# Cross-attention key loop: full-height matmuls on a block-diagonal query matrix, or 64-row tiles in pairs

## Chip, cores and metric

The kernel runs on one core of a Trainium2 chip. The metric is the device time of one execution in microseconds.

## The reference

One Perceiver-like layer on `x` [1, 128, 256], with a context of 12544 rows of 256. It has four parts. The first is nearly all of the time.

```python
q = LN(x) @ Wq.T + bq; k = ctx @ Wk.T + bk; v = ctx @ Wv.T + bv      # 128 queries, 12544 keys
scores = einsum('bhqd,bhkd->bhqk', q * 0.25, k)                      # 16 heads of 16
x += softmax(scores) @ v @ Wo.T + bo
x += linear attention of LN(x) (feature map exp / x + 1, gate)       # 128 x 256
x += causal attention with RMS norm and rope, then its MoE (8 experts, top 2, silu gate)
```

All in fp32.

## The kernel before

The context comes transposed, in 49 steps of 256 keys (`SK`). Matrices are split into a high and a low part in fp32r, and each projection is the sum of three products (high x high, low weight x high, high x low context).

For a step n the order of work is:

- `context_high(n)` (ScalarE, line 363) rounds the context to fp32r, `context_low(n)` (GpSimd, line 316) takes the rest.
- `keys(n, ...)` (TensorE, line 556) gives the keys in `k_bank`: 12 matmuls of 128x128 weights and 256 columns. `values(n, ...)` (line 567) gives the values in `v_bank`, 12 too.
- `keys_high(n)` (ScalarE, line 373) and `keys_low(n)` (VectorE, line 930) split the keys into `kst`. Six DMAs of SP (`keys_place`, line 244) lay them into a ring `kT`, so that each pair of heads takes 128 rows: 64 rows a head, of which 16 hold the high part, 16 the low part, 16 the high part again and the rest ones.
- `values_out(n)` copies the values into a ring `val`. This is ScalarE's in the first steps (line 383), VectorE's from then on (line 940).
- `max_scores(n, p)` (TensorE, line 584), for each of 8 pairs of heads: two matmuls with `qM`, one for each head. `qM` holds a head's 64 rows and zeros in the other 64. VectorE reduces the 512 results of a pair to two maxima per query (`step_max`, line 946). The two maxima banks are used in turn.
- A block is 4 steps. After its last step `block_max(b)` reduces the steps' maxima, `turn_max(b)` transposes them on TensorE into `k_bank`, VectorE's `max_turned(b)` copies them into `maxT`, and two small DMAs of SP (`max_rows`, line 257) put them, negated and in two parts, into rows of the query matrix `qmat[b % 2]`. So the scores come with the block's maximum subtracted.
- `scores(n, q)` (TensorE, line 608) runs `LAG` = 5 steps behind the maxima: 8 units of two matmuls of 256 columns, each with keys as weights and two heads of `qmat` (half zeros) as moving data. Three score banks are used in turn. ScalarE takes the exponential of a unit (`exponential`, line 403).
- `weighted_values(n, j)` (TensorE, line 624) adds the weighted values: 64 matmuls a step with 17 columns of weights (16 values and a one), four of them beside each other in columns of the array.

The order on TensorE is written out in the loop over t (lines 690 to 719): eight turns q, each with one scores unit, one maxima unit and half a projection; after the second turn stand the weighted values of the step before. In steps 49 to 53 only scores, weighted values and the turning of the blocks' parts (`turn_part`, line 647) are left. SP's order is that of lines 274 to 286: a context load, the rows of a finished block (`max_rows`), then `keys_place(t + 2)`, which waits for the slot of the ring to be free. Each engine and each queue works strictly in order.

After the loop come the merge of the 12 blocks' parts, and the small layers (lines 720 on), which the change does not touch.

Of the kernel before, what the change touches and what calls it, by code (L numbers as in the profile page):

```python
# [27 lines left out]
RING = 7  # L28
VRING = 8
CRING = 4  # L30
GROUPS = 4
# [25 lines left out]
def last_step(b):  # L57
# [11 lines left out]
    "v_done",  # L69
    "val_ready",  # L70
# [34 lines left out]
def perceiver_layer(nc, dr, out):  # L105
    ctx = ExitStack()
    with ctx:
# [43 lines left out]
        qmat = [place(f"qmat{i}", [P, PAIRS, 2, P], F32R) for i in range(2)]  # L151
        qM = place("qM", [P, PAIRS, 2, P], F32R)
# [49 lines left out]
        B = [ctx.enter_context(nc.psum_tensor(f"bank{i}", [P, 512], F32)) for i in range(8)]  # L202
        k_bank, v_bank, mx_bank, sc_bank, pv_bank = B[0], B[1], B[2:4], B[4:7], B[7]

# [19 lines left out]
        def _(sp):  # L224
# [23 lines left out]
            def max_rows(b):  # L248
# [6 lines left out]
                for a in range(2):  # L255
                    row = 64 * a + 3 * HD
                    sp.dma_start(qmat[b % 2][row:row + 2, :, a, :].bitcast(F32),
                                 maxT[2 * PAIRS * a:2 * PAIRS * (a + 1), :].bitcast(F32)
                                 ).then_inc(S["max_rows"], 16)
# [14 lines left out]
            for t in range(-2, NS + 1):  # L274
                if CRING <= t + 6 < NS:
                    ctx_load(t + 6)
                for b in range(NB):
                    if t == last_step(b) + 1:
                        max_rows(b)
                if t + 2 < NS:  # L280
                    keys_place(t + 2)
# [5 lines left out]
                if t == NS - 2:  # L287

                    sp.wait_ge(S["v_done"], 2 * NS)
# [22 lines left out]
        def _(pool):  # L312
# [6 lines left out]

            def key_ones(r):  # L320
# [3 lines left out]
            def queries(b):  # L324
# [4 lines left out]
                pool.tensor_copy(qmat[b][:, :, :, :], qM[:, :, :, :]).then_inc(S["pool_qmat"], 1)  # L329
# [4 lines left out]
            pool.memset(qM[:, :, :, :].bitcast(F32), 0.0)  # L334
# [4 lines left out]
            for t in range(-2, NS):  # L339
                if t + 3 < NS:  # L340
                    context_low(t + 3)
# [15 lines left out]
        def _(act):  # L357
            def context_high(n):

                act.wait_ge(S[f"ld_ctx{n % CRING}"], 16 * (n // CRING) + 16)  # L360
                if n >= 2:
                    act.wait_ge(S["v_done"], 2 * (n - 2) + 2)
# [14 lines left out]
            def values_out(n):  # L377


                act.wait_ge(S["v_done"], 2 * n + 2)  # L380
# [24 lines left out]

            def part_out(b):
# [17 lines left out]
            for a in range(2):  # L424
                rows = slice(64 * a, 64 * a + 64)
                last = act.activation(qM[rows, PAIRS // 2:PAIRS, a, :],
                                      mx_bank[1][rows, :].rearrange("p (h q) -> p h q", q=P), ACT.Copy)
            last.then_inc(S["act_q0"], 1)
# [4 lines left out]
            for t in range(LAST + 2):  # L433
                if t == NS:
# [4 lines left out]
                for q in range(8):  # L439
                    n = t - LAG  # L440
                    if 0 <= n < NS:
                        exponential(n, q)
                    if q == 0 and t + 2 < NS:
                        keys_high(t + 2)
                    if q == 5 and t + 2 <= LAG:
                        values_out(t + 2)
                    if q == 5 and t + 4 < NS:
                        context_high(t + 4)
                    if q == 2:
                        for b in range(NB):  # L450
                            if n - 1 == last_step(b) and t != NS:
                                part_out(b)
# [69 lines left out]
        def _(pe):  # L522
# [16 lines left out]
            def keys(n, t, half):  # L539

                if (t, half) == (0, 0):
# [4 lines left out]
                    if n >= 1:  # L546
                        turned = [b for b in range(NB) if last_step(b) == n - 4]
                        if turned:
                            pe.wait_ge(S["mt_read"], turned[0] + 1)
                        else:  # L550
                            pe.wait_ge(S["kl_ready"], n)
# [9 lines left out]
            def values(n, j, half):  # L561
# [7 lines left out]
                if half == 1:  # L569
# [6 lines left out]
            def max_scores(n, p):  # L576

                m = 8 * n + p
                if m >= 2:
                    pe.wait_ge(S["mx_read"], m - 1)  # L580
                for a in range(2):
                    if p == 2 and a == 1 and n + 3 < NS:
                        pe.wait_ge(S["cl_ready"], n + 4)
                    last = pe.matmul(mx_bank[p % 2][:, a * SK:(a + 1) * SK], qM[:, p, a, :], kT[:, n % RING, p, :],  # L584
                                     start=True, stop=True)
                last.then_inc(S["mx_done"], 1)

            def turn_max(b):
# [3 lines left out]
                pe.wait_ge(S["kl_ready"], min(last_step(b) + 4, NS))  # L592
                pe.transpose(k_bank[:, 0:P].bitcast(F32R), maxparts[:, :, :, :].rearrange("q a s p -> q (a s p)"),
                             ident_r[:, :]).then_inc(S["mt_done"], 1)

            def scores(n, q):

                k, b, j, g = 8 * n + q, block_of(n), q // GROUPS, q % GROUPS
                if n == first_step(b) and q == 0:
                    pe.wait_ge(S["max_rows"], 32 * (b + 1))  # L600
                if k >= 3:
                    pe.wait_ge(S["exp_ready"], k - 2)
                for i in range(2):
                    p = 2 * g + i
                    if q == 0 and i == 1 and n + LAG < NS:

                        keys_placed(n + LAG)
                    last = pe.matmul(sc_bank[k % 3][:, i * 2 * P:(i + 1) * 2 * P], kT[:, n % RING, p, j * P:(j + 1) * P],  # L608
                                     qmat[b % 2][:, p, :, :], start=True, stop=True)
                last.then_inc(S["sc_done"], 1)  # L610
# [690 lines left out]
```

## Time and profile before

| | |
|---|---|
| runs | 575.61 us median of 3 (575.16 to 578.5) |
| profiled execution | span 577.4 us |
| TensorE matmuls busy | 544.8 us (94%) |
| VectorE / ScalarE / GpSimd busy | 421.6 / 330.7 / 92.1 us |
| granted TensorE clock | 0.985 of full on average |
| DMA | 70.41 MB, mean 122 GB/s |

Matmuls are pipelined: a matmul's shown duration (284 ns for 256 columns) holds its way through the array, and the distance between the starts of two tells what one costs the stream. TensorE's weight loads have rows of their own (PEld) and run beside the matmuls.

### The profile page before, as it was taken

The numbers are of one execution on the slowest core, as the hardware profiler recorded it, in microseconds if no ns is written. First come the engines' busy times: TensorE is split into PE (matmuls) and PEld (weight loads), VectorE is DVE, ScalarE is ACT, GpSimd is POOL, SyncE is SP. The second block draws the span as 40 slices with busy tenths as digits, with TensorE's granted clock in tenths as the row PEclk, the third lists the DMA queues.
The fourth block names the chain that finished last, engine by engine and source line by source line (L and its number), as shares of the span: only waits on it lengthen the run. The fifth ranks groups of instructions, "written<-read, shape, count | busy, mean of one in ns | idle before, by whom it ended". The sixth has DMA issues, their size and how long they took to land.

```text
span 577.4 us, 15741 instructions
## 1 busy us (share of the span) xinstructions
PE 544.8 (94%) x6460; PEld 502.4 (87%) x6460; DVE 421.6 (73%) x797; ACT 330.7 (57%) x635; POOL 92.1 (16%) x75
## 2 busy tenths in 40 slices
PE   7888989999999999999999999999998998778897
PEld 7777989999999999999999999999987877736686
DVE  5689868778777787787787877877877317866674
ACT  3423747667676676675666766766764850062463
POOL 7641101011011011110110111101000000015000
PEclk9999999999999999999999999999999999978899
DMA  6999995856977878777678787796575019920000
GB/s 196 152 158 152 182 154 97 120 119 120 129 120 115 128 121 124 118 113 129 119 114 128 121 122 118 120 125 101 78 118 175 3 38 377 375 87 1 1 1 9
DMA packets 44615, 70.41 MB, mean 122 GB/s; under 512 B 6784, under 2 KB 15104, under 8 KB 44416
## 3 DMA queue, kind: packets, MB, share of 16 engines
q1 hardware_dynamic: 44304, 69.02, 65.8%
q8 instruction: 50, 0.82, 0.8%
q10 hardware_dynamic: 240, 0.39, 0.5%
q14 instruction: 21, 0.17, 0.1%
HBM read 30.53 MB, written 0.13 MB: 53 GB/s over the span
## 4 chain that ended last, share of the span: by engine, by line
PE 80%; DVE 8%; DMA 6%; SPq 2%; ACT 1%; issue 1%; POOL 0%; DVEq 0%
PE bank L608 17%; PE bank L624 15%; PE bank L584 14%; PE bank L567 10%; PE bank L556 10%; DMA kT<-kst 5%; PE bank L834 3%; PE bank L850 3%; SPq L244 2%; PE bank L632 2%; DVE stepmax L946 1%; DMA qmat<-maxT 1%; PE bank L654 1%; PE bank L532 1%; PE bank L647 1%
## 5 line engine op out<-in xcount | busy, mean ns | idle before, releaser
L946 DVE TENSOR_REDUCE stepmax<-bank 128x2 f32<-128x512 f32 x392 | 262.9, 688 | 92.2 <-PE bank L584 68.7
L403 ACT ACTIVATE probs<-bank 128x512 f32<-128x512 f32 x392 | 229.8, 601 | 139.8 <-PE bank L608 135.6
L608 PE MATMUL bank<-qmat,kT 128*128 128x256 f32 x784 | 164.5, 294 | 4.2 <-DMA kT<-kst 3.4
L584 PE MATMUL bank<-kT,qM 128*128 128x256 f32 x784 | 161.2, 287 | 4.1 <-DVE stepmax L946 1.9
L608 PEld LDWEIGHTS bank<-qmat,kT 128*128 128x128 f32 x784 | 120.8, 191 | 18.9 <-issue 9.9
L584 PEld LDWEIGHTS bank<-kT,qM 128*128 128x128 f32 x784 | 121.5, 191 | 7.7 <-DVE stepmax L946 4.0
L316 POOL TENSOR_TENSOR cparts<-ctxT,cparts 128x512 fp32r<-128x512 f32 x49 | 63.4, 1294 | 326.7 <-ACT cparts L363 326.6
L556 PE MATMUL bank<-cparts,wk 128*128 128x256 f32 x588 | 101.3, 283 | 2.1 <-POOL cparts L316 2.1
L567 PE MATMUL bank<-wv,cparts 128*128 128x256 f32 x588 | 101.9, 284 | 0.7 <-ACT val L383 0.7
L624 PE MATMUL bank<-probs,val 128*17 128x128 f32 x3136 | 95.1, 273 | 0.0
L624 PEld LDWEIGHTS bank<-probs,val 128*17 128x17 f32 x3136 | 81.4, 97 | 6.5
L556 PEld LDWEIGHTS bank<-cparts,wk 128*128 128x128 f32 x588 | 83.9, 191 | 2.8 <-POOL cparts L316 2.7
L567 PEld LDWEIGHTS bank<-wv,cparts 128*128 128x128 f32 x588 | 83.9, 191 | 0.9 <-ACT val L383 0.9
L373 ACT ACTIVATE kst<-bank,kbias 128x256 fp32r<-128x256 f32 x98 | 40.9, 472 | 16.2 <-DMA kT<-kst 10.4
L930 DVE SCALAR_TENSOR_TENSOR kst<-bank,kbias,kst 128x256 fp32r<-128x256 f32 x98 | 42.5, 475 | 3.0 <-ACT kst L373 3.0
L363 ACT ACTIVATE cparts<-ctxT 128x512 fp32r<-128x512 f32 x49 | 30.5, 622 | 3.2 <-PE bank L567 3.2
L940 DVE COPY val<-bank 128x512 f32<-128x512 f32 x43 | 29.2, 680 | 0.0
L352 POOL TENSOR_TENSOR low<-w,high 128x512 fp32r<-128x512 f32 x8 | 10.0, 1304 | 108.0 <-ACT high L476 108.0
L1031 DVE TENSOR_TENSOR small<-bank,bmax 128x272 f32<-128x272 f32 x11 | 4.9, 441 | 20.7 <-PE bank L647 20.6
L632 PE MATMUL bank<-const 128*128 128x128 f32 x136 | 19.8, 295 | 0.0
L834 PE MATMUL bank<-high,tparts 128*128 128x512 f32 x64 | 19.6, 429 | 0.2 <-DVE tparts L1171 0.2
L632 PEld LDWEIGHTS bank<-const 128*128 128x128 f32 x136 | 18.8, 211 | 0.3
(188 smaller groups left out, 320.7 us busy)
## 6 DMA issues: line engine op xcount, KB each, us to landing
kT<-kst SPq DMA_DIRECT2D x291, 128.0 KB, 4.6
ctxT<-in_ctxT SPq DMA_DIRECT2D x49, 256.0 KB, 5.5
w<-in_w SPq DMA_DIRECT2D x24, 512.0 KB, 10.0
bias<-in_biases SPq DMA_DIRECT2D x1, 1024.0 KB, 7.3
kT<-kst ACTq DMA_DIRECT2D x3, 128.0 KB, 5.0
qmat<-maxT SPq DMA_DIRECT2D x24, 8.0 KB
w_xk<-in_w_xk SPq DMA_DIRECT2D x1, 256.0 KB, 3.1
w_xq<-in_w_xq SPq DMA_DIRECT2D x1, 256.0 KB, 3.6
```

What stands on the lines that cost most here:

```text
L316: pool.tensor_tensor(cparts[n % 2][:, 1, :, :], ctxT[n % CRING][:, :, :], cparts[n % 2][:, 0, :, :].bitcast(F32), ALU.subtract).then_inc(S ...
L373: last = act.activation(kst[n % 2][:, 0, t * SK:(t + 1) * SK], k_bank[:, t * SK:(t + 1) * SK], ACT.Identity, bias=kbias[:, t:t + 1])
L403: act.activation(probs[k % PROBS][:, :, :], sc_bank[k % 3][:, :].rearrange("p (h q) -> p h q", q=P), ACT.Exp).then_inc(S["exp_ready"], 1)
L556: last = pe.matmul(k_bank[:, t * SK:(t + 1) * SK], wk[:, pw, c, t * P:(t + 1) * P], cparts[n % 2][:, pc, c, :], start=(i == 0), stop=(i == 5))
L567: last = pe.matmul(v_bank[:, j * D:(j + 1) * D], cparts[n % 2][:, pc, c, j * P:(j + 1) * P], wv[:, pw, c, :], start=(i == 0), stop=(i == 5))
L584: last = pe.matmul(mx_bank[p % 2][:, a * SK:(a + 1) * SK], qM[:, p, a, :], kT[:, n % RING, p, :], start=True, stop=True)
L608: last = pe.matmul(sc_bank[k % 3][:, i * 2 * P:(i + 1) * 2 * P], kT[:, n % RING, p, j * P:(j + 1) * P], qmat[b % 2][:, p, :, :], start=Tru ...
L624: last = pe.matmul(pv_bank[32 * r:32 * r + VW, g * P:(g + 1) * P], val[:, n % VRING, j, GH * g + r, :], probs[(GROUPS * ch + g) % PROBS][: ...
L632: pe.matmul(B[6][:, 0:P], ident, ident, start=True, stop=True)
L834: last = pe.matmul(B[2 * which + i][:, :], tparts[:, a, c, :], weights, start=(n == 0), stop=(n == len(products) - 1))
L930: last = dve.scalar_tensor_tensor(kst[n % 2][:, 1, cols], k_bank[:, cols], kbias[:, t:t + 1], kst[n % 2][:, 0, cols].bitcast(F32), ALU.add ...
L946: dve.tensor_reduce(stepmax[:, n - first_step(block_of(n)), 2 * p:2 * p + 2], mx_bank[p % 2][:, :].rearrange("p (a k) -> p a k", a=2), AX_ ...
```

## The change

The key loop works with 64-row tiles. `qM` and `qmat` lose their zeros (`[P, PAIRS, P]`): head pairs lie above each other, 64 rows each, and two matmuls of 64 rows each, one in the upper and one in the lower half of the array, take the place of one full-height matmul. Scores have 4 units of 8 matmuls of 128 columns, over two banks, and maxima 4 units of 4 matmuls of 256 columns, over two adjacent banks that VectorE reads with one instruction. The projections are done in row halves, keys in one half and values in the other, and then swapped (`project_both`). `LAG` stays 5; the ring of keys has 8 slots, that of values 10.

Other moves: the values are always copied by ScalarE; the high part of the context comes from GpSimd from step 4 on; the turned maxima go through `v_bank` and ScalarE; in SP's order `keys_place` stands before `max_rows`; TensorE waits for the rows in the first maxima unit of the step in which the block's scores begin; the values of step 2 are projected ahead of the loop.

```diff
-RING = 7
-VRING = 8
+RING = 8
+VRING = 10
+EARLY = 3
+UNITS = 4
...
-        qmat = [place(f"qmat{i}", [P, PAIRS, 2, P], F32R) for i in range(2)]
-        qM = place("qM", [P, PAIRS, 2, P], F32R)
+        qmat = [place(f"qmat{i}", [P, PAIRS, P], F32R) for i in range(2)]
+        qM = place("qM", [P, PAIRS, P], F32R)
...
+        mx = ctx.enter_context(nc.psum_tensor("maxima", [P, 1024], F32))
+        mx_bank = [mx[:, 0:512], mx[:, 512:1024]]
...
@@ SP
                 if CRING <= t + 6 < NS:
                     ctx_load(t + 6)
+                if t + 2 < NS:
+                    keys_place(t + 2)
                 for b in range(NB):
                     if t == last_step(b) + 1:
                         max_rows(b)
-                if t + 2 < NS:
-                    keys_place(t + 2)
...
@@ GpSimd
+            def context_high(n):
+                pool.wait_ge(S[f"ld_ctx{n % CRING}"], 16 * (n // CRING) + 16)
+                pool.wait_ge(S["k_done"], n - 1)
+                pool.wait_ge(S["v_done"], n - 1)
+                pool.tensor_copy(cparts[n % 2][:, 0, :, :], ctxT[n % CRING][:, :, :]).then_inc(S["ch_ready"], 1)
...
@@ ScalarE
+                if t + 2 < NS:
+                    keys_high(t + 2)
+                    values_out(t + 2)
+                for b in range(NB - 1):
+                    if t == last_step(b) + 1:
+                        max_turned(b)
+                for b in range(NB):
+                    if n - 1 == last_step(b) and t != NS:
+                        part_out(b)
+                if 0 <= n < NS:
+                    for q in range(8):
                         exponential(n, q)
...
@@ TensorE
+            top, low = slice(0, 64), slice(64, 128)
+
+            def project_both(n, swapped, first, end):
+                for i in range(first, end):
+                    t, (pw, pc, c) = i // 6, products[i % 6]
+                    k_rows, v_rows = (low, top) if swapped else (top, low)
...
+                        return pe.matmul(k_bank[:, cols], wk[k_rows, pw, c, t * P:(t + 1) * P], cparts[n % 2][k_rows, pc, c, :],
+                                         start=begin, stop=finish, skip_group_check=True)
...
+                        return pe.matmul(v_bank[:, cols], cparts[n % 2][v_rows, pc, c, t * P:(t + 1) * P], wv[v_rows, pw, c, :],
+                                         start=begin, stop=finish, skip_group_check=True)
+                    if swapped:
+                        if i == 0:
+                            pe.wait_ge(S["half_done"], n - EARLY + 1)
+                        if i == 8:
+                            keys_placed(n - 2)
+                        v_last, k_last = values_product(), keys_product()
...
+            def maxima(n, m):
+                if m == 0 and (n == 0 or n + 2 >= NS):
+                    keys_placed(n)
+                if UNITS * n + m >= 1:
+                    pe.wait_ge(S["mx_read"], UNITS * n + m)
+                for i in range(2):
+                    p = 2 * m + i
+                    if i == 1:
+                        if m == 1 and n + 3 < NS:
+                            pe.wait_ge(S["cl_ready"], n + 4)
+                        for b in range(NB):
+                            if m == 0 and n == first_step(b) + LAG:
+                                pe.wait_ge(S["max_rows"], 32 * (b + 1))
+                    for a, rows in enumerate((top, low)):
+                        last = pe.matmul(mx_bank[a][:, i * SK:(i + 1) * SK], qM[rows, p, :], kT[rows, n % RING, p, :],
+                                         start=True, stop=True)
                 last.then_inc(S["mx_done"], 1)
...
+            def scores(n, s):
+                b, j, half = block_of(n), s // 2, s % 2
+                k = 8 * n + 2 * s
...
+                if k >= 2:
+                    pe.wait_ge(S["exp_ready"], k - 1)
+                for r in range(GH):
+                    p = GH * half + r
+                    for a, rows in enumerate((top, low)):
+                        last = pe.matmul(sc_bank[(k + a) % 3][:, r * P:(r + 1) * P], kT[rows, n % RING, p, j * P:(j + 1) * P],
+                                         qmat[b % 2][rows, p, :], start=True, stop=True)
+                        if r == GH - 1:
+                            last.then_inc(S["sc_done"], 1)
...
+                if t < NS:
+                    maxima(t, 0)
+                    if 0 <= n - 1:
+                        weighted_values(n - 1, 0)
+                        weighted_values(n - 1, 1)
+                    for b in range(NB - 1):
+                        if t == last_step(b) + 1:
+                            turn_max(b)
+                    if 0 <= n:
+                        scores(n, 0)
+                    maxima(t, 1)
+                    if t + 3 < NS:
+                        project_both(t + 3, False, 0, 8)
+                    if 0 <= n:
+                        scores(n, 1)
+                    maxima(t, 2)
+                    if t + 3 < NS:
+                        project_both(t + 3, False, 8, 12)
+                    if 0 <= n:
+                        scores(n, 2)
+                    if t + 3 < NS:
+                        project_both(t + 3, True, 0, 4)
+                    maxima(t, 3)
+                    if 0 <= n:
+                        scores(n, 3)
+                    if t + 3 < NS:
+                        project_both(t + 3, True, 4, 12)
+                    continue
...
@@ VectorE
+            def step_max(n, m):
+                dve.wait_ge(S["mx_done"], UNITS * n + m + 1)
+                heads = stepmax[:, n - first_step(block_of(n)), :].rearrange("q (a p) -> q a p", a=2)
+                dve.tensor_reduce(heads[:, :, 2 * m:2 * m + 2],
+                                  mx[:, :].rearrange("p (a i k) -> p a i k", a=2, i=2), AX_X, ALU.max
                                   ).then_inc(S["mx_read"], 1)
...
+            for t in range(NS + 1):
                 for b in range(NB):
                     if t == last_step(b) + 1:
                         block_max(b)
+                if t == NS:
+                    last_max_turned()
+                if t < NS:
+                    for m in range(UNITS):
+                        step_max(t, m)
+                        if m == 0 and t + 2 < NS:
+                            keys_low(t + 2)
```

In the prediction M0 to M3 are the maxima units of a step, S0 to S3 its scores units. In steps 49 to 53 the four scores units stand one behind the other, after the weighted values and two turned parts follow the first.

## Rows read from the trace of the kernel before

**Rows 1.** The page, busy us, share of the span and instructions by engine.

```profile
PE 544.8 (94%) x6460; PEld 502.4 (87%) x6460; DVE 421.6 (73%) x797; ACT 330.7 (57%) x635; POOL 92.1 (16%) x75
```

**Rows 2.** The page, chain of work that ended last, shares of the span by line.

```profile
PE bank L608 17%; PE bank L624 15%; PE bank L584 14%; PE bank L567 10%; PE bank L556 10%; DMA kT<-kst 5%; PE bank L834 3%; PE bank L850 3%; SPq L244 2%; PE bank L632 2%; DVE stepmax L946 1%; DMA qmat<-maxT 1%; PE bank L654 1%; PE bank L532 1%; PE bank L647 1%
```

**Rows 3.** Timeline of one step: start, length (us), instruction, count, [idle before, releaser].

```profile
250.94 1.94 PE L624 MATMUL bank<-probs,val 128*17 128x128 f32 x64
...
252.81 0.50 PE L608 MATMUL bank<-qmat,kT 128*128 128x256 f32 x2
...
253.15 0.40 PE L584 MATMUL bank<-kT,qM 128*128 128x256 f32 x2
...
253.59 0.69 DVE L946 TENSOR_REDUCE stepmax<-bank 128x2 f32<-128x512 f32 x1 [1.43 <-PE bank L584]
...
253.75 0.40 PE L608 MATMUL bank<-qmat,kT 128*128 128x256 f32 x2
...
259.72 1.94 PE L624 MATMUL bank<-probs,val 128*17 128x128 f32 x64
```

**Rows 4.** Timeline, weighted values that bound stretches, and a turned part.

```profile
63.38 1.94 PE L624 MATMUL bank<-probs,val 128*17 128x128 f32 x64
...
442.82 1.94 PE L624 MATMUL bank<-probs,val 128*17 128x128 f32 x64
...
454.85 0.60 PE L647 MATMUL bank<-const,parts 128*128 128x128 f32 x4
...
455.92 1.94 PE L624 MATMUL bank<-probs,val 128*17 128x128 f32 x64
...
461.38 1.94 PE L624 MATMUL bank<-probs,val 128*17 128x128 f32 x64
...
471.31 1.94 PE L624 MATMUL bank<-probs,val 128*17 128x128 f32 x64
```

**Rows 5.** Timeline, weight loads of eight transposes ahead of the loop.

```profile
15.38 0.74 PEld L676 LDWEIGHTS bank<-ident_r,qparts 128*128 128x128 f32 x8 [1.11 <-issue]
```

**Rows 6.** Groups by line: count, busy us, mean ns, idle us before, releaser.

```profile
L946 DVE TENSOR_REDUCE stepmax<-bank 128x2 f32<-128x512 f32 x392 | 262.9, 688 | 92.2 <-PE bank L584 68.7
L403 ACT ACTIVATE probs<-bank 128x512 f32<-128x512 f32 x392 | 229.8, 601 | 139.8 <-PE bank L608 135.6
...
L930 DVE SCALAR_TENSOR_TENSOR kst<-bank,kbias,kst 128x256 fp32r<-128x256 f32 x98 | 42.5, 475 | 3.0 <-ACT kst L373 3.0
L373 ACT ACTIVATE kst<-bank,kbias 128x256 fp32r<-128x256 f32 x98 | 40.9, 472 | 16.2 <-DMA kT<-kst 10.4 <-PE bank L556 5.8
...
L1210 DVE TENSOR_TENSOR low<-w,high 128x1024 fp32r<-128x1024 f32 x4 | 4.9, 1222 | 2.6 <-ACT high L476 2.6
...
L329 POOL CAST qmat<-qM 128x2048 fp32r<-128x2048 f32 x2 | 3.8, 1894 | 0.0
```

**Rows 7.** Timeline of the first steps: the first maxima, and maxima that wait for VectorE.

```profile
21.87 0.40 PE L584 MATMUL bank<-kT,qM 128*128 128x256 f32 x2
...
24.30 3.85 DVE L946 TENSOR_REDUCE stepmax<-bank 128x2 f32<-128x512 f32 x6
...
25.04 0.50 PE L584 MATMUL bank<-kT,qM 128*128 128x256 f32 x2 [0.36 <-DVE stepmax L946]
```

**Rows 8.** Timeline of SP's issues: two steps' keys, and a block's rows.

```profile
248.83 3.76 SPq L244 DMA_DIRECT2D kT<-kst  x6
...
257.61 4.47 SPq L244 DMA_DIRECT2D kT<-kst  x6
...
263.28 1.34 SPq L257 DMA_DIRECT2D qmat<-maxT  x2
```

**Rows 9.** Chain in order of time: start and length of those rows' landing.

```profile
263.97 3.18 DMA qmat<-maxT
```

**Rows 10.** Line 244, from the issue of a keys' transfer to its landing.

```profile
DMA to landing us min/median/max: 3.2/4.6/8.1
```

**Rows 11.** Line 257, who waited for the blocks' rows: us, times.

```profile
  PEld bank L608: 1.2, 4
```

More of the change, by code:

```diff
@@ L423, in _ @@
             act.wait_ge(S["pe_qT"], 2)
[L424 to L428, printed above, removed]
+            act.activation(qM[:, PAIRS // 2:PAIRS, :], mx_bank[1][:, :].rearrange("p (h q) -> p h q", q=P), ACT.Copy
+                           ).then_inc(S["act_q0"], 1)
             values_out(0)
@@ L546, in keys @@
                     if n >= 1:
[L547 to L551, printed above, removed]
+                        pe.wait_ge(S["kl_ready"], n)
                 for i in range(3 * half, 3 * half + 3):
@@ L591, in turn_max @@
                 pe.wait_ge(S["mparts_ready"], 2 * b + 2)
-                pe.wait_ge(S["kl_ready"], min(last_step(b) + 4, NS))
-                pe.transpose(k_bank[:, 0:P].bitcast(F32R), maxparts[:, :, :, :].rearrange("q a s p -> q (a s p)"),
+                if b < NB - 1:
+                    pe.wait_ge(S["val_ready"], last_step(b) + 4)
+                else:
+                    pe.wait_ge(S["kl_ready"], NS)
+                bank = v_bank if b < NB - 1 else k_bank
+                pe.transpose(bank[:, 0:P].bitcast(F32R), maxparts[:, :, :, :].rearrange("q a s p -> q (a s p)"),
                              ident_r[:, :]).then_inc(S["mt_done"], 1)
-            def scores(n, q):
-                k, b, j, g = 8 * n + q, block_of(n), q // GROUPS, q % GROUPS
-                if n == first_step(b) and q == 0:
+            def scores(n, s):
+                b, j, half = block_of(n), s // 2, s % 2
+                k = 8 * n + 2 * s
+                if n == first_step(b) and s == 0 and n + LAG >= NS:
                     pe.wait_ge(S["max_rows"], 32 * (b + 1))
[L601 to L610, printed above, removed]
+                if k >= 2:
[7 more added lines that the diff above has]
+                            last.then_inc(S["sc_done"], 1)
             def weighted_values(n, j):
@@ L689, in _ @@
             pe.wait_ge(S["act_q0"], 1)
+            for j in range(2):
+                for half in range(2):
+                    values(2, j, half)
             for t in range(LAST + 2):
                 n = t - LAG
+                if t < NS:
[26 more added lines that the diff above has]
+                    continue
                 if t == NS:
```

157 lines of the change are left out of this document (70 added, 87 removed).

## The prediction

> **What bounds the kernel now.** I read the busy shares first: TensorE 94%, VectorE 73%, ScalarE 57% [rows 1]. The chain of waits, by line, says the same: the matmul lines 608, 624, 584, 567 and 556 hold most of it, kT's transfers 5% [rows 2]. So the key loop is a TensorE stream, and the timeline of one step shows its price [rows 3]. From the weighted values of one step (250.94) to those of the next (259.72) are 8.78 us. From 253.15 to 253.75 lie five 256-column matmuls, 0.12 us each. A step has 16 for the scores, 16 for the maxima and 24 for the projections: 56 x 0.12 = 6.72. The 64 small matmuls of the weighted values take 1.87 (250.94 to 252.81), the first matmul after them shows its weight load (0.50 instead of 0.40), 0.10. That is 8.69; the 0.09 left stand ahead of them, at the change of the array's shape. Over the loop, from the weighted values of step 6 to those of step 49, it is 442.82 - 63.38 = 379.4 for 43 steps [rows 4], 8.82 each.
>
> **The matmuls.** In before, scores and maxima multiply by a block-diagonal query matrix, so half of each product is with zeros. Afterwards each matmul takes 64 rows, and two stand in the array together. Pairs per step: maxima 8 (256 columns), scores 16 (128 columns), projections 24 (256 columns). No row shows two row tiles side by side. The nearest is the weighted values: four column tiles of 128 columns, 4 x 1.87/64 = 0.117 per four, about the price of one 256-column matmul [rows 3]. So I take 0.12 for a 256-column pair; from below nothing suggests less, since 256 columns in one tile take that; from above it is two loads in a row, 2 x 0.085 (next paragraph) = 0.17.
>
> A scores pair streams only 128 columns but loads 128. Eight transposes of that form have their loads in 0.74 us, the last of them taken at some 0.14 by itself, so (0.74 - 0.14)/7 = 0.085 apart [rows 5]; the bounds are 0.085 and 0.12. Sixteen pairs are 1.36 to 1.92. The Trainium skill ("TensorE: Matmul & The Clock Gate", LDWEIGHTS) says that a load's time goes by its columns, columns/1.2 ns, whatever the rows: 107 ns, which speaks against any gain in the scores. The row's 0.085 is shorter, and the row decides; by the page's figure the step would be only some 0.09 longer, since the other three scores units lie under the wait of the next paragraph.
>
> TensorE alone would then need (8 + 24) x 0.12 + 1.4 to 1.9 + 2.06 = 7.3 to 7.8 us per step, 1.0 to 1.5 less than now.
>
> **The maxima's round trip takes part of that.** The maxima now fill both banks in one unit, and a unit waits until VectorE has read the one before. In before there were two banks in turn. The round trip: 0.44 from the first matmul to VectorE's start (253.15 to 253.59 [rows 3]), a reduction of 1024 elements 1.22 (512 take 0.688, and the 1024-element row says 1.222 [rows 6]), 0.05 back to TensorE (24.30 + 0.69 to 25.04 [rows 7]). That is 1.71; a unit that waited shows its load (0.50 instead of 0.40 [rows 7]), then 1.81. TensorE's own work between two units is 0.24 + 0.96 + scores 0.34 to 0.48 = 1.54 to 1.68, in all three gaps without weighted values. So all three are set by VectorE: 1.71 + 1.81 + 1.81. The fourth gap, 0.34 + 0.09 + 1.87 + 0.10 + 0.34 to 0.48, is 2.74 to 2.88. Together 8.07 to 8.21, I take 8.14, plus the 0.04 by which the mean now stands above 8.78: 8.18. Middle of the loop: 43 x (8.82 - 8.18) = **-27.7**.
>
> **Other moves, costed at nothing in the loop.** VectorE then has 4 x 1.22 + 0.87 = 5.8 a step; the values' copy goes to ScalarE, which loses the context's high part in return (both 512 elements, like the exponential's 0.60) and has 9 x 0.60 + 2 x 0.47: 6.3 of 8.2 [rows 6]. Scores units of two banks wait for the first exponential of the last unit: 0.65 + 0.04 + 0.60 + 0.04 = 1.33, under the 1.71 of the maxima. GpSimd's copy of 512 elements lies between a quarter of the 1.89 that 2048 take and that whole 1.89, on an engine 16% busy [rows 1, 6]; it can run a whole step ahead. The cover of ScalarE's and VectorE's work on keys and values is the time until the projection behind M1; its slack is some 0.3 us, and what they are later than that TensorE waits.
>
> **The maxima's rows in SP's queue.** This decides. Every fourth step the block maxima go by two small DMAs into qmat. With eight slots of kT instead of seven SP no longer waits for the step's scores before the keys' transfers, and sends them as soon as keys_low is done. The change moves them behind the six transfers of keys_place, and moves TensorE's wait for them to the second pair of the first maxima unit (M0) of the next step, with everything of that step queued behind it. Count from M0 of the step that issues them. keys_low is two instructions of 0.475 [rows 6], 0.87 with their overlap, and ends at 0.54 + 1.22 + 0.87 = 2.6. The six issues take 3.76 to 4.47 [rows 8]: 7.1. The two small ones, first issue to landing: 263.28 to 263.97 + 3.18 = 267.15, 3.87 [rows 8, 9]: 11.0. TensorE asks at 8.14 + 0.12 = 8.26. It waits **2.75 us**, ten times in this stretch: **+27.5**. From below: six issues in 3.76, 2.05. From above: the second small DMA, issued at 7.8, lands like a kT transfer, 4.6 later [rows 10]: 4.2. In before the rows go first and land just in time: the lines that wait for them lose 1.2 us in all [rows 11].
>
> **Start.** Twelve value matmuls are moved ahead of the loop, +1.4. Without scores and weighted values the step goes by VectorE's chain: 0.54 + 1.22 + 0.87 (keys_low) + 1.22 + 2 x (0.05 + 0.54 + 1.22) + 0.05 = 7.5. Now six such steps and 0.9 take 63.38 - 21.87 = 41.5 [rows 4, 7], 6.8 each. So 6 x 0.7 = 4.2, and the first block's own wait for its rows, 2.75, falls here too: **+8.4** (5 to 11).
>
> **End.** With maxima and projections gone (steps 49 to 53) scores came bank by bank, 455.92 to 461.38 = 5.46 a step with two turned parts [rows 4]. Now the scores units follow each other at 1.33, three times, with ScalarE idle while unit 0, the weighted values (2.06) and both parts' turns (2 x about 0.45: 0.60 less the last one's way through the array [rows 4]) run: 4.0 + 0.44 + 2.06 + 0.9 = 7.4; without turns 6.5. Over 28.5 us of now (442.82 to 471.31) I get 35: **+7** (5 to 9).
>
> **Sum.** 577.4 - 27.7 + 27.5 + 8.4 + 7 = 592.6. The profiled span is 1.8 above the median of the runs (575.61), so I forecast 591. Its own range: with the step at 8.11 (-30.5), waits of 2.05 and both ends cheap (+10), 576; with 8.25 (-24.5), waits of 4.2 and +20, 613.
>
> **Rivals.**
> (1) The rows land in time, since SP issues faster, or TensorE reaches its question later: 592.6 - 27.5 - 2.75 - 1.8 = 560 (552 to 572). For it: before loses almost nothing to them. Against: 2.6 + 3.76 + 3.87 is 10.2, and every number in it is a measured row; it needs a step over 10 us.
> (2) Row tiles do not run side by side: two loads of 0.085 per pair, 48 x 0.17 + 2.06 = 10.2 a step, +60 in 43; the rows' wait shrinks to 0.7 a block, +7, and start and end stay, +15: 577.4 + 82 - 1.8, some 658. Pairs of 0.15 make 9.26 a step (+19) and waits of 1.6 (+16): 626. For it: no row shows row tiles. Against: the column tiles. The Trainium skill (the same page, Part 3) lets a load overlap running matmuls only where the row groups differ. The trace does not agree: full-height loads are hidden under full-height matmuls at 0.12; by that rule load and matmul would stand one behind the other, some 0.2 a pair, and the result would lie beyond this rival's 658.
> (3) The wait is at its lower end and start and end cost less than worked out, or the step is at 8.0: gain and loss nearly cancel. With 8.0 (-35), waits of 2.05 and +10 it is 571; the band is 570 to 581.
>
> **Numbers.** Forecast's mechanism 0.45, a twentieth of it within 1%; rival 1 0.28; rival 2 0.15; rival 3 0.12. About 1% of 575.6 is what a measurement of this kernel tells from no change. Faster: most of rival 1 and a little more, 0.30. Same: 0.15. Slower: 0.55. The range runs from inside rival 1 to the end of the forecast's own, 557 to 615; left out are some 0.08 below and 0.11 above.
>
> **What would show it.** Matmul starts of the projections 0.06 apart, scores pairs 0.09 to 0.12. Idle time of the maxima's line before it, released by stepmax, some 0.1 to 0.3 three times a step, and by the transfer qmat<-maxT, 2 to 4 us every fourth step at M0. Steps without it 8.1 to 8.2. Reductions of 1.22 x 196. In steps 49 to 53 scores waiting for probs. Wrong if no idle time stands before the maxima from qmat, or if projection starts lie 0.08 or more apart.

## The result, and the profile after

The changed kernel takes 658.5 us (657.6 to 660.9), the one before 576.4 in the same measurement: a ratio of 1.144, interval 1.140 to 1.149. The prediction said 591, 557 to 615. The sign was right, the size was not. Of the executions reported below, two of e6's six (its profiled one among them), one of e8's four and one of e10's six ran in a slower state, and the ratios leave them out.

The page of the changed kernel has less TensorE in its span than before [rows 1], 86% against 94%, and VectorE 59%. So something waits.

```profile
PE 569.5 (86%) x8348; PEld 490.0 (74%) x8348; DVE 388.5 (59%) x546; ACT 326.9 (50%) x643; POOL 117.3 (18%) x120
```

The slices show what the prediction had no term for. TensorE's granted clock was full nearly everywhere in the kernel before (0.985 on average); now it is 0.894, with dips all along and a trough near the end (slices of the kernel before, then of the changed one):

```profile
PEclk9999999999999999999999999999999999978899
PEclk9988698989989799897989979899777675987899
```

The timeline of TensorE around one block's rows, projections left out (columns as in [rows 3]):

```profile
260.49 0.29 PE L647 MATMUL maxima<-kT,qM 64*128 64x256 f32 x2
263.81 0.58 PE L647 MATMUL maxima<-kT,qM 64*128 64x256 f32 x2 [3.03 <-DMA qmat<-maxT]
264.32 3.26 PE L692 MATMUL bank<-probs,val 128*17 128x128 f32 x64
...
273.86 1.94 PE L692 MATMUL bank<-probs,val 128*17 128x128 f32 x64
...
282.08 1.94 PE L692 MATMUL bank<-probs,val 128*17 128x128 f32 x64
```

M0's first two matmuls run, its second two wait 3.03 us for the rows: the wait of the prediction, at its place. But then the same 64 matmuls of the weighted values that need 1.94 take 3.26, and the step from 264.32 to 273.86 takes 9.54, where the next takes 8.22. Stretches of the same time show why (length; busy us and instructions of PE, PEld, DVE, ACT, POOL; granted clock, DMA share, GB/s): clock 0.65 right behind the wait, 1.00 from 268.3 on.

```profile
257.00:260.00 3.00, 3.00 (x48) 2.75 (x48) 2.11 (x2) 2.47 (x5) 0.00 (x0) 1.00 0.70 139
260.00:264.30 4.30, 1.27 (x16) 0.87 (x12) 0.34 (x1) 2.05 (x5) 1.87 (x2) 0.93 0.74 125
264.30:268.30 4.00, 4.00 (x80) 3.21 (x79) 2.01 (x3) 0.65 (x2) 0.00 (x0) 0.65 0.10 34
268.30:272.00 3.70, 3.70 (x62) 3.46 (x60) 2.45 (x2) 2.88 (x6) 0.00 (x0) 1.00 0.93 145
```

SP's issues before that wait, to hold beside [rows 8]: six keys' transfers, then the block's rows.

```profile
255.31 4.62 SPq L250 DMA_DIRECT2D kT<-kst  x6
260.04 1.35 SPq L263 DMA_DIRECT2D qmat<-maxT  x2
```

Who waited for whom, in all (us, times, longest): the rows in all eleven blocks, 35.3/11 = 3.2 us each. Ten of the eleven lie in the 43 steps, 2.9 to 4.1 us long, 32.5 together. The other two lines are the maxima's waits for VectorE.

```profile
PE maxima L647 <- DMA qmat<-maxT: 35.3, 11, 4.1
PEld maxima L647 <- DVE stepmax L1028: 19.6, 29, 1.7
PE maxima L647 <- DVE stepmax L1028: 16.1, 28, 1.6
```

Where the 81.7 us between the profiled spans (577.4, 659.1) lie, by the weighted values of steps 6, 49 and 54 (after: 77.87, 503.68, 553.23; before: [rows 4]): the start +14.5 (forecast +8.4), the 43 steps +46.4 (forecast 0), the end +21.1 (forecast +7), the rest nothing.

The steps without a block's maximum show the maxima's round trip. A unit starts, VectorE's reduction starts 0.54 later and takes 1.23, and the next unit starts 0.05 behind it: 1.82 in all.

```profile
249.30 0.50 PE L647 MATMUL maxima<-kT,qM 64*128 64x256 f32 x4
249.84 1.23 DVE L1028 TENSOR_REDUCE stepmax<-maxima 128x4 f32<-128x1024 f32 x1 [0.60 <-PE maxima L647]
251.12 0.50 PE L647 MATMUL maxima<-kT,qM 64*128 64x256 f32 x4
```

### The profile page after: what moved, and what is told of

It is laid out like the page before. It is cut to its first block, busy times and chain, and to the rows that moved or that the text cites. A ratio compares the mean times of both kernels' runs of the same rounds, so it can differ in the third digit from the quotient of the medians.

```text
span 659.1 us, 19306 instructions
## 1 busy us (share of the span) xinstructions
PE 569.5 (86%) x8348; PEld 490.0 (74%) x8348; DVE 388.5 (59%) x546; ACT 326.9 (50%) x643; POOL 117.3 (18%) x120
## 4 chain that ended last, share of the span: by engine, by line
PE 64%; DVE 18%; SPq 8%; DMA 5%; ACT 2%; issue 2%; POOL 0%; DVEq 0%
PE bank L692 15%; PE bank L675 11%; PE maxima L647 10%; PE bank L604 8%; DVE stepmax L1028 7%; SPq L250 7%; PE bank L614 7%; DMA qmat<-maxT 5%; PE bank L940 2%; DVE bmax L1046 2%; DVE kst L1020 2%; PE maxima L924 2%; PE bank L924 1%; ACT probs L418 1%; PE bank L700 1%
## 5 line engine op out<-in xcount | busy, mean ns | idle before, releaser
L1028 DVE TENSOR_REDUCE stepmax<-maxima 128x4 f32<-128x1024 f32 x196 | 239.6, 1222 | 185.8 <-PE maxima L647 185.7
L604 PE MATMUL bank<-cparts,wk 64*128 64x256 f32 x1104 | 172.4, 290 | 4.2 <-DVE kst L1020 4.2
L614 PE MATMUL bank<-wv,cparts 64*128 64x256 f32 x1104 | 172.5, 291 | 0.3
L604 PEld LDWEIGHTS bank<-cparts,wk 64*128 64x128 f32 x1104 | 148.6, 193 | 7.6 <-DVE kst L1020 7.6
L614 PEld LDWEIGHTS bank<-wv,cparts 64*128 64x128 f32 x1104 | 148.7, 193 | 1.6 <-PE bank L614 1.6
L647 PE MATMUL maxima<-kT,qM 64*128 64x256 f32 x784 | 102.6, 337 | 51.6 <-DMA qmat<-maxT 35.3
L675 PE MATMUL bank<-qmat,kT 64*128 64x128 f32 x1568 | 127.3, 284 | 10.8 <-ACT probs L418 10.8
L675 PEld LDWEIGHTS bank<-qmat,kT 64*128 64x128 f32 x1568 | 110.8, 199 | 27.0 <-ACT probs L418 13.5
L647 PEld LDWEIGHTS maxima<-kT,qM 64*128 64x128 f32 x784 | 64.2, 199 | 70.5 <-DMA qmat<-maxT 37.5
L332 POOL CAST cparts<-ctxT 128x512 fp32r<-128x512 f32 x45 | 27.5, 611 | 331.9 <-PE bank L604 331.9
L323 POOL TENSOR_TENSOR cparts<-ctxT,cparts 128x512 fp32r<-128x512 f32 x49 | 62.7, 1281 | 12.7 <-ACT cparts L378 9.1
L388 ACT ACTIVATE kst<-bank,kbias 128x256 fp32r<-128x256 f32 x98 | 41.1, 470 | 39.6 <-PE bank L604 33.9
L398 ACT ACTIVATE val<-bank 128x512 f32<-128x512 f32 x49 | 29.4, 599 | 2.7 <-PE bank L581 2.7
```

What stands on the lines that cost most here:

```text
L323: pool.tensor_tensor(cparts[n % 2][:, 1, :, :], ctxT[n % CRING][:, :, :], cparts[n % 2][:, 0, :, :].bitcast(F32), ALU.subtract).then_inc(S ...
L388: last = act.activation(kst[n % 2][:, 0, t * SK:(t + 1) * SK], k_bank[:, t * SK:(t + 1) * SK], ACT.Identity, bias=kbias[:, t:t + 1])
L604: return pe.matmul(k_bank[:, cols], wk[k_rows, pw, c, t * P:(t + 1) * P], cparts[n % 2][k_rows, pc, c, :], start=begin, stop=finish, skip_ ...
L614: return pe.matmul(v_bank[:, cols], cparts[n % 2][v_rows, pc, c, t * P:(t + 1) * P], wv[v_rows, pw, c, :], start=begin, stop=finish, skip_ ...
L647: last = pe.matmul(mx_bank[a][:, i * SK:(i + 1) * SK], qM[rows, p, :], kT[rows, n % RING, p, :], start=True, stop=True)
L675: last = pe.matmul(sc_bank[(k + a) % 3][:, r * P:(r + 1) * P], kT[rows, n % RING, p, j * P:(j + 1) * P], qmat[b % 2][rows, p, :], start=Tr ...
```

## Experiments

Times are medians, with the ratio to the kernel before and its interval. A and B are the theory and the rival of each expectation. Steps are distances between weighted values in the profile.

**e1_rows_first.**

```diff
+                for b in range(NB):
+                    if t == last_step(b) + 1:
+                        max_rows(b)
                 if t + 2 < NS:
                     keys_place(t + 2)
-                for b in range(NB):
-                    if t == last_step(b) + 1:
-                        max_rows(b)
```

> The changed kernel with one edit: in SP's order the block's rows (max_rows) stand ahead of the keys' transfers again. Theory A (the wait for the rows, and behind it the lower TensorE clock, are the loss in the loop): TensorE no longer waits for qmat at M0 (72.8 us of idle rows before, 11 blocks), the granted clock stays 1.0 from the weighted values of step 6 to those of step 49, every step is 8.22 us, so this stretch takes 43 x 8.25 = 355 us instead of 425.8; with the first block's wait gone too the run is at 578 to 590. Rival B (the clock falls because a step of 64-row work with its three short waits per step is not dense enough, waits or not): the clock stays near 0.9 in the loop, only the 37 us of waits go, 620. The last steps (49 to 54) stay at 49 us under both.

600.6 us, 1.040 (1.033 to 1.047): 58 less than the changed kernel, by the place of two small DMAs. No wait for qmat is left and the clock is 1.00 from step 6 to step 45, as A has it, and B falls with it. The total is above A's 578 to 590. The 43 steps take 369.7 us, not 355: a step with a block's maximum takes 9.27, the others 8.22, and steps 46 to 48 take 8.9, 10.4 and 10.9. 56.1 us went in the 43 steps. The ten waits in them were 32.5, so some 23.6 are left for the clock behind the waits. 19.7 of it can be seen directly, in the steps behind the waits, which took 9.54 to 10.60 instead of 8.22.

**e2_filled_wait.**

```diff
                             if m == 0 and n == first_step(b) + LAG:
+                                for _ in range(32):
+                                    for a, rows in enumerate((top, low)):
+                                        pe.matmul(mx_bank[a][:, i * SK:(i + 1) * SK], qM[rows, p, :],
+                                                  kT[rows, n % RING, p, :], start=True, stop=True)
                                 pe.wait_ge(S["max_rows"], 32 * (b + 1))
```

> The changed kernel with one edit: ahead of the wait for the rows in M0 TensorE repeats the second pair of that maxima unit 32 times (3.8 us of matmuls whose results are overwritten), so that it is busy while the rows are on their way. The wait itself is as long as before. Theory A (a part of the loss is the clock that falls behind the wait): the rows land at the same time, but the clock stays 1.0 in the loop, so that the steps behind a wait take 8.2 us and not 9.5 to 10.6; 11 blocks x some 3 us less, 620 to 632. Rival B (the wait is all of the loss, the clock only follows the idle time): 655 to 662.

644.3 us, 1.113 (1.104 to 1.122), between A (620 to 632) and B (655 to 662). The mechanism is A's. The fill takes 3.94 us, longer than the wait it covers, and behind it the weighted values run at full speed:

```profile
295.07 0.29 PE L651 MATMUL maxima<-kT,qM 64*128 64x256 f32 x2
...
299.01 0.28 PE L651 MATMUL maxima<-kT,qM 64*128 64x256 f32 x2
299.22 0.96 PE L696 MATMUL bank<-probs,val 128*17 128x128 f32 x28
```

The step behind is 8.22. Four steps take 37.8 instead of 39.6 on average (steps 9 to 45). A's size was too large because the fill (3.94) is longer than most of the waits (2.9 to 4.1), and because the clock had cost the step behind a wait 1.3 to 2.4 us and not 3. Adding 704 matmuls to a kernel makes it 14 us faster.

**e3_late_copy.** `block_max` of the changed kernel ends with a copy of 16 elements. In the kernel before, the instruction that writes the same tile took 0.17. On VectorE and GpSimd the timeline of the changed kernel reads:

```profile
251.35 0.61 POOL L332 CAST cparts<-ctxT 128x512 fp32r<-128x512 f32 x1 [6.25 <-PE bank L604]
251.40 0.59 DVE L1042 TENSOR_SCALAR maxparts<-curmax 128x16 fp32r<-128x16 f32 x1
...
252.03 0.18 DVE L1044 SCALAR_TENSOR_TENSOR maxparts<-curmax,maxparts 128x16 fp32r<-128x16 f32 x1
252.04 1.30 POOL L323 TENSOR_TENSOR cparts<-ctxT,cparts 128x512 fp32r<-128x512 f32 x1
252.12 1.26 DVE L1046 COPY bmax<-curmax 128x16 f32<-128x16 f32 x1
...
253.29 1.21 DVE L1028 TENSOR_REDUCE stepmax<-maxima 128x4 f32<-128x1024 f32 x1
...
254.43 0.86 DVE L1020 SCALAR_TENSOR_TENSOR kst<-bank,kbias,kst 128x256 fp32r<-128x256 f32 x2
```

Both slow small instructions end within 0.04 us of the GpSimd instruction that they started under. M0's reduction (253.29) and `keys_low` (254.43) stand behind them. The edit:

```diff
                 for m in range(UNITS):
                     step_max(t, m)
                     if m == 0 and t + 2 < NS:
                         keys_low(t + 2)
+                    for b in range(NB - 1):
+                        if m == 1 and t == last_step(b) + 1:
+                            keep_max(b)          # the copy, taken out of block_max(b)
```

> The changed kernel with one edit: VectorE's copy of the block maxima into bmax stands behind the second maxima unit's reduction instead of ahead of the first. In the changed kernel it takes 1.26 us in a step's start, ending with GpSimd's subtraction, where 16 elements took 0.17 in the kernel before. Theory A (it waits for GpSimd, which now works at that moment, and so delays the keys, their transfers and the rows behind them): moved, it takes 0.17 again, the rows land 1.2 us earlier in each of 11 blocks, the wait for them falls from some 3.3 to 2.1, the run gets 12 to 25 us shorter, 634 to 648. Rival B (the copy's form with its permuted elements is slow by itself): it takes 1.26 wherever it stands; the rows still land earlier, but the next reduction is 1.1 later; 640 to 655 and mean of that line unchanged.

641.1 us, 1.111 (1.102 to 1.120), inside the ranges of both. The copy itself tells them apart, for A: all twelve take 0.17, where the median was 1.26:

```profile
L1049 DVE COPY bmax<-curmax x12: 164/165/169, 59.6 to 484.3; 128x16 f32<-128x16 f32 x12
```

Same form, same operands, another moment: it was GpSimd. The changed kernel agrees without any edit. Its twelfth copy, the only one with no GpSimd instruction beside it, takes 0.17 in the old place:

```profile
502.62 0.17 DVE L1042 TENSOR_SCALAR maxparts<-curmax 128x16 fp32r<-128x16 f32 x1
...
502.92 0.17 DVE L1046 COPY bmax<-curmax 128x16 f32<-128x16 f32 x1
```

The waits for the rows fall to 31.6/11 = 2.9 only, not to A's 2.1. `keys_low` ends 1.2 earlier, and the rows land 0.8 to 2.1 earlier, but M0's reduction comes earlier too, and with it TensorE asks for the rows 0.85 earlier. The 43 steps get 18.3 us shorter: 12.7 lie in the ten steps that end with a wait and 7.1 in the steps behind them, where the clock was low; steps 46 to 48 give 1.5 back. The Trainium skill ("SBUF — State Buffer", "Who interferes with whom") says that copies and tensor_scalar of VectorE can take the pair of ports that it shares with GpSimd, which one instruction holds to its end while the other engine's blocks. These rows agree.

**e4_three_edits.** Rows first, late copy, and in steps 49 to 54:

```diff
@@ in words
-                    scores(0), weighted values 0 and 1, two turned parts, scores(1), scores(2), scores(3)
+                    scores(0), weighted values 0, scores(1), weighted values 1, scores(2), a part, scores(3), a part
```

> The changed kernel with three edits: rows first (as in the run of that name), late copy (as in that run), and in steps 49 to 54 the scores units are spaced out by the other work: scores 0, weighted values 0, scores 1, weighted values 1, scores 2, a turned part, scores 3, a turned part. Theory A (the end is long because three scores units stand behind each other at 1.35 us while ScalarE idles during everything else, and because TensorE is then at half clock): these steps fall from 10.3 to 5.4 to 6.5 us, the end from 49.6 to 28 to 35, and with the rows first the run is at 558 to 568, faster than the kernel before. Rival B (the clock is low there whatever the order, because the exponentials bound): the end stays above 42, 572 to 580.

574.0 us, 0.994 (0.991 to 0.998). The end falls from 49.6 to 32.2 us, as A has it, with three steps of 5.87. B's reason falls, though the total lies in B's range and not in A's: steps 46 to 48 stay at 8.9, 10.5 and 10.9, and step 49 at 10.0, at a clock of 0.66 to 0.88. The 43 steps take 362.3 us, 7.4 less than in e1. That is the late copy, since a block's step now takes 8.44 and not 9.27.

**e5_split_values.** On e4, the order of a step (and ScalarE's copy of a block's part behind its second exponential):

```diff
@@ in words
-    M0 values0 values1 S0 | M1 proj8 S1 | M2 proj4 S2 proj4 | M3 S3 proj8
+    M0 values0 S0 | M1 values1 S1 | M2 proj8 S2 proj4 | M3 proj4 S3 proj8
```

> The kernel of e4_three_edits with the loop's order on TensorE changed: the weighted values' two halves stand behind M0 and behind M1, and the projection moves behind M2 and M3 (ScalarE's copy of a block's part behind its second exponential). Theory A (the round trip of the maxima, 1.8 us for each of three gaps in which TensorE has less work than that, sets 8.22 us a step): every gap now holds more than 1.8 us of TensorE work, the step falls to TensorE's own sum, 24 x 0.118 + 4 x 0.29 + 4 x 0.40 + 1.87 + 2 x 0.19 = 7.85 us (7.8 to 8.0), 43 x 0.35 = 12 to 15 us less, 559 to 563. Rival B (TensorE's own stream is the 8.22, the idle times before maxima are not the bound): each more change of the array's shape costs 0.2, the step is 8.3 to 8.5, 577 to 586.

566.2 us, 0.982 (0.976 to 0.988), between A and B. The step is 8.06, neither 7.85 nor 8.3. A is right that the round trip had set 8.22 (the work is the same and a change of shape more). Of the gain expected in the 43 steps, 12 to 15 us, 5.3 come. A plain step has no idle time ahead of a unit. It is A's prices that were low: the weighted values need 2 x 1.00 and not 1.87, the projections 3.04 and not 2.83, since each stay between scores loses some 0.05 to 0.1. A step with a transpose takes 8.62, with 0.31 of idle time ahead of the transpose, for ScalarE's copy of the values.

**e6_full_height.** On e4, the projections as 24 full-height matmuls in the same four places, the keys' twelve first. M0 then asks in each step whether its keys have landed, which costs no idle time in the stretch below.

```diff
@@ abridged
-    pe.matmul(k_bank[:, cols], wk[k_rows, ...], cparts[n % 2][k_rows, ...])     # 24 pairs
+    pe.matmul(k_bank[:, cols], wk[:, ...], cparts[n % 2][:, ...])               # 24
```

> The kernel of e4_three_edits with one part undone: the projections are full-height matmuls again (24 of 256 columns instead of 24 pairs of 64 rows), in the same places. Theory A (row pairs cost TensorE what one full-height matmul costs, 0.118; the point of the halves is to keep the array's shape, and a change costs some 0.1 to 0.2 of which the waits for VectorE hide a part): six more changes of shape a step, of which the gap behind M1 has no room and the others 0.1 each; the step goes to 8.4 to 8.9, the run to 582 to 604. Rival B (full-height and row matmuls follow each other without loss): the step stays 8.22, the run 572 to 577.

613.2 us, 1.062 (1.055 to 1.069). Its step is 9.11, above A's range, at full clock and with no idle time shown:

```profile
250.00:300.00 50.00, 50.00 (x740) 42.66 (x731) 32.21 (x40) 31.45 (x63) 9.80 (x11) 1.00 0.73 115
```

```profile
251.15 0.45 PE L671 MATMUL maxima<-kT,qM 64*128 64x256 f32 x4
251.53 1.21 PE L645 MATMUL bank<-cparts,wk 128*128 128x256 f32 x8
252.68 0.66 PE L699 MATMUL bank<-qmat,kT 64*128 64x128 f32 x8
```

The maxima units stand 2.0 to 2.3 apart where no weighted values lie between, above the 1.82 of the round trip, so TensorE's own stream sets this step. Eight full-height matmuls need 1.15 from start to the next unit's start, eight pairs 8 x 0.118 = 0.94 (0.118 is the distance of pairs averaged over a stretch of them): 0.2 on leaving the other shape. Entering it costs about 0.1 (a maxima unit to the first of them 0.38, to the first pair 0.29), so a stay costs some 0.3. A step has four such stays. So the row halves are needed, though by themselves they save nothing. The Trainium skill ("TensorEngine Tiling (Array Packing)", Tiling Modes) says that changing the mode drains the array; the rows, with a loss at each change, agree.

**e7_filled_ends.** On e4:

```diff
                     if 0 <= n:
                         scores(n, 0)
+                    else:
+                        filler(t, 8, (sc_bank[0], sc_bank[1]))           # results not read
...
                     if t + 3 < NS:
                         project_both(t + 3, False, 0, 8)
+                    else:
+                        fill_end(t, 8)                                   # as many pairs, into k_bank and v_bank
```

> The kernel of e4_three_edits with matmuls added whose results nobody reads: in steps 46 to 48, which have no projection, as many pairs in the same places, and in steps 0 to 4, which have no scores, 8 pairs between M0 and M1. Theory A (the clock falls to 1.2 GHz there because TensorE idles some 0.3 to 0.8 us before each maxima unit, and then the step is 10.5 instead of 8.2): with more work the clock stays 1.0 and steps 46 to 48 take 8.2 each, 5 to 7 us less; in the first steps VectorE sets the time, and the maxima units at full clock give 1 to 4 us more: 563 to 569. Rival B (the low clock there has another cause, or VectorE's chain hides it): 573 to 580, since the added work takes time.

568.7 us, 0.985 (0.978 to 0.993), A. Steps 46 to 48 take 8.32, 8.32 and 8.87. The 43 steps take 356.6 (e4: 362.3), which is the price of the loop at full clock.

**e8_split_filled.** e5 and e7 together.

> Both edits, e5_split_values and e7_filled_ends, on the kernel of e4_three_edits. Theory A for both: the gains add up, steps at 7.85 to 7.95 from 6 to 48 and full clock, 550 to 558, clear of the kernel before. Rival B: they overlap, since with the weighted values split the last steps are denser anyway, 559 to 565.

565.4 us, 0.983 (0.976 to 0.991), at the edge of B's range. The reason is not B's: in e5 steps 47 and 48 still took 10.3 and 10.7. On top of e7 the split gives only 3.2 us in the 43 steps, since the plain step falls from 8.22 to 8.06 but a block's step rises from 8.43 to 8.62. Single runs lie between 561 and 570.

**e9_old_end_order.** On e7, steps 49 to 54 in the changed kernel's order again.

> The kernel of e7_filled_ends (568.7) with one part undone: in steps 49 to 54 the order is again that of the changed kernel (scores 0, weighted values, two turned parts, then three scores units). TensorE comes into these steps at full clock, since steps 46 to 48 are filled. Theory A (the order alone costs the 7 us of the prediction, and the rest of the changed kernel's 49.6 us is half clock that it carries in from steps 46 to 48): the steps take 7.4 and the end 35, 571 to 574. Rival B (the order makes the low clock itself, by the 0.7 us that TensorE idles ahead of each of three scores units): the clock falls within the first of these steps, they take 10.3, the end 45 to 50, 582 to 588.

583.8 us, 1.009 (1.006 to 1.012): B. TensorE comes in at full clock (1.00 up to 434.15), and by 435.56 it is at half (0.50), within the first of these steps:

```profile
432.80 0.66 PE L688 MATMUL bank<-qmat,kT 64*128 64x128 f32 x8 [0.68 <-ACT probs L418]
434.15 0.74 PE L688 MATMUL bank<-qmat,kT 64*128 64x128 f32 x8 [0.68 <-ACT probs L418]
435.56 1.11 PE L688 MATMUL bank<-qmat,kT 64*128 64x128 f32 x8 [0.68 <-ACT probs L418]
436.61 3.61 PE L705 MATMUL bank<-probs,val 128*17 128x128 f32 x64
```

The units follow each other at 1.35 (forecast 1.33), TensorE idling 0.68 of each, and the third and the weighted values then run at half speed. The order makes its own clock.

**e10_later_turn.** On e8, `turn_max` behind the second half of the values, ScalarE's copy of it behind the second exponential.

> The kernel of e8_split_filled (565.4) with the block's transpose moved behind the second half of the weighted values, and ScalarE's copy of it behind the step's second exponential. In e8 a step with a transpose takes 8.62 instead of 8.06, and TensorE idles 0.3 us ahead of the transpose for ScalarE's copy of the values. Theory A: that idle time goes, ten steps of 8.3, 562 to 564. Rival B: the copy behind the exponential delays the third scores unit or the projection's start by as much: no change, 564 to 567.

566.7 us, 0.980 (0.975 to 0.985). A block's step falls from 8.62 to 8.28, as A has it, yet the run is no shorter. In its profiled execution the start is 3.8 us longer than in e8's, at a clock of 0.80 from 55 us on, and the end 2.9, at 0.90, where e8's has 1.00 in both. Whether the edit or chance brings that, these runs don't tell. Of all versions e5, e8 and e10 are the fastest, 2% under the kernel before. They are not told apart, and e7's interval overlaps theirs.

## Why the prediction was wrong

**Right.** Row tiles run side by side. The timeline of TensorE in the changed kernel shows pairs of 256 columns (the two lines of a pair are its two halves):

```profile
250.43 0.28 PE L614 MATMUL bank<-wv,cparts 64*128 64x256 f32 x1
250.44 0.28 PE L604 MATMUL bank<-cparts,wk 64*128 64x256 f32 x1
250.55 0.28 PE L614 MATMUL bank<-wv,cparts 64*128 64x256 f32 x1
250.56 0.28 PE L604 MATMUL bank<-cparts,wk 64*128 64x256 f32 x1
```

Both halves start within 0.01, the next pair 0.12 later. The loads of the pair at 250.55 start at 250.44, as the pair at 250.43 begins to run:

```profile
250.44 0.19 PEld L614 LDWEIGHTS bank<-wv,cparts 64*128 64x128 f32 x1
250.44 0.19 PEld L604 LDWEIGHTS bank<-cparts,wk 64*128 64x128 f32 x1
```

The Trainium skill ("TensorE: Matmul & The Clock Gate", Part 3) lets a load overlap running matmuls only where the row groups differ. These rows do not agree: the next pair's loads are of the same two row groups as the pair that runs.

The plain step is 8.22 (forecast 8.14, or 8.18 with what was added for the mean), set by the maxima's round trip of 1.82 (forecast 1.81), as e5 shows. The wait for the rows stands where it was put, in eleven blocks, and e1 shows that SP's order is its cause. The end's rhythm was 1.35 for 1.33.

**Wrong: every term was priced at full clock.** The sum has no term for the clock, and nothing in it asks what a wait does to the matmuls behind it. Of the 67 us between forecast and time 46 lie in the 43 steps, 14 in the end and 6 in the start. The 43 steps, forecast -27.7 + 27.5 = 0, measured +46.4:

| term | forecast | measured | from |
|---|---|---|---|
| steps at full clock | -27.7 | -22.8 | 356.6 (e7) - 379.4 |
| ten waits for the rows | +27.5 | +32.5 | 2.9 to 4.1 each |
| clock behind the waits | none | +23.6 | e1: 56.1 less the waits |
| VectorE held by GpSimd | none | +7.4 | 369.7 (e1) - 362.3 (e4) |
| low clock, steps 46 to 48 above all | none | +5.7 | 362.3 (e4) - 356.6 (e7) |

The clock's +23.6 is what is left over and takes up whatever else changed with the waits; 19.7 of it was seen in the steps behind them. In the first line, 4.9 short of the forecast, the plain step is 0.04 above the mean that was forecast, and neither the 0.2 of a block's step at full clock nor the 8.3 to 8.9 of steps 46 to 48 had a term.

**Mis-sized: the end.** +7 was forecast for steps of 7.4; they took 10.7, 10.5, 10.4, 9.8 and 8.2, +21.1. The order makes the low clock itself (e9): what was taken from [rows 3] as 2.06 for the weighted values took 3.6.

**Mis-sized: the wait.** 2.75 became 2.9 to 4.1. Both ends of it moved. Counted from M0 of the block's step, `keys_low` ended at 4.2 (forecast 2.6) and the rows landed at 12.6 to 13.7 (11.0), but TensorE asked at 9.7 (8.26). The cause of both is the start of VectorE's step. `block_max` with its two held instructions stands ahead of M0's reduction, and the prediction had it at nothing: M0's reduction starts 2.2 behind M0 (251.12 to 253.29) and not 0.54. The move of the context's high part to GpSimd was costed at nothing. That was true of GpSimd, and wrong of VectorE, which now meets it there. With the copy moved (e3) these are 3.0, 11.5 to 12.0 and 8.8, and the waits 2.7 to 3.2.

**The start**: +14.5 for +8.4. The first block's wait is in it with its clock: e1 has 5.3 us less there. The clock is low there too, 0.82 from 21.87 to 77.87 (before: 1.00). In e8, whose first steps are filled and run at 1.00, the start is +5.3. The rest was not taken apart.

**The offset.** I took 1.8 off because the profiled span stood that much above the runs' median. But the profiled execution of the changed kernel took 660.9 with a span of 659.1, so a run stands 1.8 above its own span. This is small beside the miss.

**The ranges.** 658 is also what rival 2 named, by loads standing one behind the other. The agreement is chance: the pairs start 0.12 apart, not 0.17. Its mechanism is refuted by the same rows that confirm that row tiles run side by side.

## What to carry to other kernels

Price a wait on a full TensorE twice: its own length, and the matmuls behind it at the lower clock; here 32.5 us of waits cost up to 23.6 more. When work moves to GpSimd, look which small VectorE instructions will now stand under it. And read each in-order queue in full when a step is moved: two small DMAs behind six larger ones were 58 of the 82 us lost. With them in front alone the changed kernel is still 4% slower than the one before. It takes the late copy, the spread end and the split values as well to make the row tiles worth 2%.

## What the runs showed of the hardware

- Behind a wait of 3.03 us the granted clock was 0.65 on average over the next 4.0 us. But no long wait is needed: idle times of 0.68 before each unit of 0.66 did it in e9 by the third unit. In the end's stretch of the changed kernel TensorE is busy 40.0 of 49.6 us at 0.67, in the kernel before 28.0 of 28.5 at 1.00, and in e4, from 450 to 462 us, 11.0 of 12.0 at 1.00.
- A 16-element VectorE copy of 0.17 us took 1.26 under a GpSimd subtraction of 1.30, and a 16-element TENSOR_SCALAR of 0.17 took 0.59 under a GpSimd cast of 0.61.
- Two row tiles of 64 rows, in different banks, cost one full-height matmul (0.118 against 0.12); a stay of full-height matmuls between units of row tiles cost some 0.3, 0.1 going in and 0.2 coming out (e6).
